# VectorE normalises the tile two slots ahead in front of a slot's activation

## What is computed

```
x = x + 0.5 * ffn(layernorm(x))
x = x + rec(layernorm(x))
x = x + 0.5 * ffn(layernorm(x))

def ffn(x):                                   # 8 experts, top 1
    p = softmax(x @ Wr + br); e = argmax(p); gate = max(p)
    h = relu((norm(x) * ln_g + ln_b) @ W1[e] + b1[e])      # 256 -> 1024
    return (h @ W2[e] + b2[e]) * gate                      # 1024 -> 256

def rec(x):                                   # in 64 features
    x = x @ down_w.T
    for l in range(3):
        c = causal convolution of 4 taps(x)
        r, i = sigmoid(c @ Wr.T + br), sigmoid(c @ Wi.T + bi)
        a = exp(8 * r * log_sigmoid(log_a))
        h_t = a_t * h_(t-1) + sqrt(1 - a_t^2) * i_t * c_t
        x = rms_norm(h @ out_w.T) * norm_w
    return x @ up_w.T
```

## Time and profile before

| | before |
|---|---|
| time of the runs, median | 835.54 us (833.80 to 836.45) |
| the profiled execution's own time | 837.64 us |
| its span in the profile | 835.8 us |
| TensorE matmul busy | 724.3 us, 87% |
| VectorE busy | 393.5 us, 47% |
| ScalarE busy | 266.0 us, 32% |
| GpSimd busy | 194.1 us, 23% |
| mean granted TensorE clock | 0.969 |

### The profile page before, as it was taken

One profiled execution on the slowest core, in us unless ns is written; L12 is line 12 of the kernel. 1 busy time (PEld: TensorE's weight loads), 2 busy tenths in 40 slices (PEclk: granted clock), 3 DMA queues, 4 the chain that ended last, 5 costly groups with the idle time before them and its releaser, 6 DMA issues.

```text
span 835.8 us, 16437 instructions
## 1 busy us (share of the span) xinstructions
PE 724.3 (87%) x4704; PEld 636.1 (76%) x4704; DVE 393.5 (47%) x1248; ACT 266.0 (32%) x670; POOL 194.1 (23%) x193
## 2 busy tenths in 40 slices
PE   5304998999979999999984999999995779999993
PEld 4204986999969878987863887888785669999993
DVE  5401465333326666677641475767774223332331
ACT  3102241222222455563400236566241122222220
POOL 4530136311112211111562130111057011111110
PEclk9999998999999999999988999999998889999998
DMA  6984575875546333342446443433324534555520
GB/s 215 324 271 160 182 232 172 258 233 197 206 140 245 133 126 128 127 138 107 122 164 215 141 162 126 135 133 118 121 90 146 178 127 143 184 187 180 190 70 10
DMA packets 65217, 136.58 MB, mean 163 GB/s; under 512 B 9157, under 2 KB 40146, under 8 KB 64980
## 3 DMA queue, kind: packets, MB, share of 16 engines
q1 hardware_dynamic: 57620, 118.37, 42.3%
q0 software_dynamic: 7488, 16.93, 5.8%
HBM read 114.10 MB, written 24.84 MB: 166 GB/s over the span
## 4 chain that ended last, share of the span: by engine, by line
PE 77%; issue 7%; SPq 6%; DVE 5%; DVEq 2%; DMA 1%; another core or an unknown queue 1%; POOL 0%; POOLq 0%
PE bank L1343 34%; PE bank L1356 30%; PE bank L1245 3%; PE bank L1330 2%; PE bank L1194 2%; SPq L346 2%; SPq L386 2%; PE bank L1250 1%; PE bank L1255 1%; PE bank L1273 1%; DMA w<-in_L_ffn_W 1%; PE bank L1237 1%; DVE act_t L908 1%; DVEq L323 1%
## 5 line engine op out<-in xcount | busy, mean ns | idle before, releaser
L1343 PE MATMUL bank<-mn_t,w 128*128 128x128 f32 x2592 | 319.9, 279 | 12.6 <-issue 12.6
L1343 PEld LDWEIGHTS bank<-mn_t,w 128*128 128x128 f32 x2592 | 307.8, 196 | 21.4 <-issue 21.2
L1356 PE MATMUL bank<-w,act_t 128*128 x1296 | 305.0, 387 | 9.7 <-DVE res L921 5.6
L1356 PEld LDWEIGHTS bank<-w,act_t 128*128 128x128 f32 x1296 | 244.4, 194 | 50.8 <-issue 20.3
L908 DVE TENSOR_SCALAR act_t<-bank,vec 128x128 f32<-128x128 f32 x324 | 91.2, 344 | 188.2 <-PE bank L1343 171.4
L1101 ACT ACTIVATE mn_t<-bank,vec 128x128 f32<-128x128 f32 x162 | 65.2, 452 | 343.7 <-PE bank L1330 282.3
L1111 ACT ACTIVATE act_t<-bank,vec 128x128 f32<-128x128 f32 x324 | 92.6, 369 | 94.0 <-PE bank L1343 81.7
L530 POOL DMA_INDIRECT out_x<-res,pay x40 | 40.8, 1020 | 278.1 <-DVE res L921 277.5
L530 POOL DMA_INDIRECT x_middle<-res,pay x41 | 41.9, 1021 | 268.1 <-DVE res L921 267.2
L915 DVE TENSOR_TENSOR y_b<-bank,b_all 128x256 f32<-128x256 f32 x81 | 34.4, 424 | 130.8 <-PE bank L1356 107.1
L1330 PE MATMUL bank<-ident,mn 128*128 128x128 f32 x162 | 32.8, 285 | 62.6 <-DVE mn L901 41.5
(11 more groups left out here) (157 smaller groups left out, 402.8 us busy)
## 6 DMA issues: line engine op xcount, KB each, us to landing
w<-in_L_ffn_W SPq DMA_DIRECT2D x89, 1024.0 KB
pay<-routed_rows SPq DMA_DIRECT2D x81, 130.0 KB, 2.1
routed_rows<-fill SPq DMA_DIRECT2D x4, 1040.0 KB, 6.2
rows<-in_L_attn_h SPq DMA_DIRECT2D x8, 512.0 KB, 4.8
rows<-x_middle SPq DMA_DIRECT2D x8, 512.0 KB, 6.2
b_all<-in_L_ffn_b SPq DMA_DIRECT2D x1, 1024.0 KB
routed_rows<-rows,dest POOLq DMA_INDIRECT x64
x_middle<-res,pay POOLq DMA_INDIRECT x41, 3.6
```

Of the source, the lines that this page charges most:

```text
L1343: last = t.matmul(b_hid[n][:, c % 4 * P:(c % 4 + 1) * P], w1[i % W1S][:, k * F + c * P:k * F + (c + 1) * P], mn_t[p % 2][i % 2][:, k * P:( ...
L1356: last = t.matmul(b_out[i % 2], act_t[i % 2][:, c * P:(c + 1) * P], w2[:, ds(eb * (WE // FC) + c * D, D)], start=c == 0, stop=c == FC - 1)
```

## The change

VectorE's `norm(p, i + 2)` is called behind `finish(p, i - 2)` and ahead of the work beside the slot and of `activate(p, i)`, in all slots; in the first seven slots it gets an `If` block of its own. The ticks of the other work are new in many places.

```diff
--- before.py
+++ after.py
@@ -21,45 +21,45 @@
 
 SUB = 8
 LN_POW = [40, 48]
-LN_NORMALISE = [96, 112]
+LN_NORMALISE = [96, 120]
 DOWN = [504, 552]
 KEEP_DOWN = [121, 137]
-LN_MOMENTS = [[72, 80], [88, 104]]
+LN_MOMENTS = [[80, 81], [88, 104]]
 LN_TRANSPOSE = [[440, 464], [505, 528]]
 LN_KEEP = [[112, 120], [128, 136]]
-UP = [[1090, 1104], [1112, 1144]]
-ADD = [[273, 275], [280, 288]]
-TAP = [[129, 138], [184, 185], [233, 240]]
-CONVOLVE = [[128, 136], [185, 192], [233, 240]]
-GATES = [[553, 584], [768, 784], [960, 992]]
-TANH = [[139, 152], [192, 200], [241, 248]]
-GATE_INPUT = [[144, 152], [193, 200], [248, 256]]
-ROOT = [[153, 160], [201, 208], [249, 264]]
-SCAN = [[160, 161], [208, 216], [257, 264]]
-PROJECT = [[672, 688], [872, 897], [1064, 1089]]
-SQUARES = [[168, 169], [216, 225], [265, 273]]
-NORMS = [[689, 704], [896, 913], [1088, 1096]]
-RMS_ROOT = [[170, 176], [224, 232], [272, 280]]
-INVERSE = [[176, 177], [224, 232], [272, 274]]
-SPREAD = [[712, 728], [912, 952]]
-RESCALE = [[178, 184], [225, 234]]
+UP = [[1080, 1105], [1112, 1136]]
+ADD = [[272, 274], [280, 282]]
+TAP = [[129, 138], [177, 184], [232, 235]]
+CONVOLVE = [[128, 136], [178, 184], [226, 248]]
+GATES = [[553, 584], [736, 768], [944, 1032]]
+TANH = [[139, 152], [185, 192], [234, 264]]
+GATE_INPUT = [[144, 152], [192, 200], [240, 264]]
+ROOT = [[153, 154], [200, 201], [248, 266]]
+SCAN = [[153, 160], [208, 216], [256, 265]]
+PROJECT = [[656, 681], [864, 889], [1048, 1088]]
+SQUARES = [[168, 170], [216, 224], [265, 272]]
+NORMS = [[680, 697], [888, 912], [1072, 1104]]
+RMS_ROOT = [[169, 176], [217, 233], [267, 280]]
+INVERSE = [[168, 177], [224, 227], [266, 273]]
+SPREAD = [[696, 728], [896, 945]]
+RESCALE = [[176, 179], [225, 232]]
 R_POW = [[56, 57], [144, 145], [144, 145]]
-R_LOGITS = [[504, 552], [1161, 1200], [1161, 1200]]
-R_KEEP_LOGITS = [[128, 138], [296, 299], [296, 299]]
-R_TURN_LOGITS = [[528, 568], [1176, 1216], [1176, 1216]]
+R_LOGITS = [[504, 552], [1152, 1176], [1152, 1176]]
+R_KEEP_LOGITS = [[128, 138], [288, 297], [288, 297]]
+R_TURN_LOGITS = [[528, 568], [1160, 1192], [1160, 1192]]
 R_CHOOSE = [[128, 144], [296, 312], [296, 312]]
-R_EXP = [[137, 152], [300, 320], [300, 320]]
-R_RANKS = [[553, 616], [1208, 1288], [1208, 1288]]
+R_EXP = [[137, 152], [304, 320], [304, 320]]
+R_RANKS = [[553, 616], [1216, 1288], [1216, 1288]]
 R_PLACE = [[136, 152], [304, 320], [304, 320]]
-R_MOMENTS = [[[104, 112], [113, 120]], [[281, 289], [290, 297]], [[281, 289], [290, 297]]]
-R_SCATTER = [[[64, 72], [80, 88]], [[152, 160], [161, 168]], [[152, 160], [161, 168]]]
-R_TRANSPOSE = [[[440, 464], [472, 529]], [[1120, 1145], [1160, 1177]], [[1120, 1145], [1160, 1177]]]
-R_KEEP = [[[112, 120], [129, 136]], [[281, 288], [297, 298]], [[281, 288], [297, 298]]]
+R_MOMENTS = [[[104, 112], [120, 121]], [[281, 288], [289, 290]], [[281, 288], [289, 290]]]
+R_SCATTER = [[[64, 72], [80, 81]], [[152, 160], [161, 168]], [[152, 160], [161, 168]]]
+R_TRANSPOSE = [[[440, 464], [472, 529]], [[1120, 1137], [1153, 1161]], [[1120, 1137], [1153, 1161]]]
+R_KEEP = [[[112, 120], [129, 136]], [[281, 282], [289, 296]], [[281, 282], [289, 296]]]
 R_COUNTS = [648, 1320, 1320]
-R_TABLES = [160, 328, 328]
+R_TABLES = [168, 328, 328]
 LAYER_COLUMNS = 48
 EXP_LOG_A = 56
-LOG_SIGMOID = 56
+LOG_SIGMOID = 64
 
 
 
@@ -940,15 +940,17 @@
                             finish(p, i - 2)
                     elif i >= 2:
                         finish(p, i - 2)
+                    if i < DYN:
+                        with dve.If(used > SLOTS - 1 - i):
+                            norm(p, i + 2)
+                    elif i + 2 < SLOTS:
+                        norm(p, i + 2)
                     beside(p, 2 * i)
                     if i < DYN:
                         with dve.If(used > SLOTS - 1 - i):
                             activate(p, i)
-                            norm(p, i + 2)
                     else:
                         activate(p, i)
-                        if i + 2 < SLOTS:
-                            norm(p, i + 2)
                     beside(p, 2 * i + 1)
                 if p == 0:
                     begin(1)
```

## The result

| | before | after |
|---|---|---|
| median, us | 835.77 (826.66 to 846.85, 20 runs) | 841.12 (834.21 to 844.16, 20 runs) |
| ratio after/before | | 1.0077, 95% interval 1.0047 to 1.0106 |
| profiled execution, us | 837.64 | 839.0 |
| its span, us | 835.8 | 837.3 |
| mean granted clock | 0.969 | 0.929 |

The kernel got slower by 0.8%, beyond the 0.3% that a measurement of it can tell. The forecast was no change at 836.3 us; 841.1 us lies inside its range, but the time moved beyond the measurement's interval where the forecast had no change.

The account below looks back on a forecast made before the run. TensorE was taken to bound the kernel, losing time only at second slots and crawls. The terms -7.04 - 0.49 + 8.3 = +0.8 us gave 836.3 us on the median, no change, range 827 to 842 us.

Parts of the forecast that it names:

- The move of the normalise: Second slot of each phase: input transposes no longer wait for the normalise, -7.04 us, plus -0.49 us in phase 0.
- late next: Second half of the following first products waits for VectorE's activation: some 1.2 us, against 2.0 us of other TensorE work.
- The new places at 0: Other work moved to new ticks on TensorE and VectorE: cost 0, bounds 0 to +2 us.
- scatter place: GpSimd, phase 0: scatters from [80, 88] to [80, 81] make a separate run of 9 issues, +8.3 us.
- The argument from busy time: Mixed slots of phases 1 and 2: TensorE almost always busy, so no idle time to win; activation has over 4 us slack.
- the line of the prediction itself: GpSimd runs of issues: a run of 9 costs 8.2 or 8.3 us, each further issue 1.1 us.
- rival D: Phase 1 or phase 0's new run: a store joins eight scatters, run of 14, 5.4 us more, 841.7 us; chance 0.16.
- Rows and branches: VectorE: waits for rows cost 0, up to 2 us per slot; 28 branch steps cost 0, at most 5.6 us.
- Case B: Phase 0: no crawl for the new run of scatters, 828.0 us or up to 830, faster; chance 0.30.
- the rule from the Trainium skill: Straight code streams ahead, so by it the longer scatter run would cost nothing; the forecast held the timeline against it.

Follow-up runs that it names:

- first set: Four kernels taking the change apart (normalise move, new places, scatter place), run on one chip beside the kernel before, which took 811.51 us there.
- before_again: The kernel before, unchanged, profiled again in the second set of runs: 811.51 us, ratio 1.0007.
- after_third: The kernel after, unchanged, run again where the kernel before took 840.14 us: 840.56 us, ratio 1.0041.
- the pair of the fourth set: The kernel after, unchanged, 840.56 us, and the same with phase 0's scatters back at ticks [80, 88] instead of [80, 81], 832.72 us.
- spread_second: Kernel before with only the normalise moved and each phase's four groups of scatters in four different slots: 829.88 us, ratio 0.9892.
- the pause: Kernel after with a drain and a 2.9 us power operation on GpSimd behind every four scatters: 880.93 us, ratio 1.052.

## Why the prediction was wrong, and where it was right

**The move of the normalise** was right in mechanism and size: forecast 7.04 us at four places, measured 1.90 + 1.83 + 1.75 + 1.94 = 7.42 us. What was called late next, the second half of the first products, waits 0.29 us in phase 1, once. Alone, it is 0.9903 where there are crawls. In the first set, without them, it is 0.9862; the intervals overlap, so that it is worth more there is not shown, though two more transposes wait for the normalise in `before_again`.

**The new places at 0** is the step that failed, and it turned the direction. The bounds were 0 to +2 us. In the profiled pair of the case the sum of 0.8 us became 5.0: the scatter place gave 1.2 us of the difference, the move -0.4 us, and all that the forecast had put at nothing 3.4 us net; its largest parts are 2.03 us in the mixed slots of phase 1 and 2.92 us in the stretch behind them. In the first set, where crawls play no part, the new places with the normalise behind cost 0.7% (5.5 us, interval 3.3 to 7.7), and with the move, and the old scatter place, 806.25 against 799.53 us, 6.7 us. The profiles of that last pair are 9.5 us apart and say where: 1.8 us in the mixed slots, 4.9 us in the stretches behind phases 1 and 2, 1.8 us up to the end of phase 0, 1.6 us in the first two slots of phase 2, the rest -0.6. The argument from busy time ("no idle time to win, and slack of over 4 us") looked at the activation, which had slack; the finish, which frees the bank of the second products, had none: TensorE waits for it 11.3 us instead of 5.6. That is shown for the moments (1.2 us in one slot); how far each of the other moved places contributes, and what delays the stretches behind the phases, was not tried. Where crawls occur, the split is less certain: 832.72 against 830.73 us, ratios whose intervals overlap.

**The scatter place** was right in mechanism and roughly in size. The text took a separate run of 9 at 8.3 us and argued that the next store would come late. In the profiled execution a store came in time on the near side (at 133.28 us) and joined the new run to the old one: 18 issues. The price follows the line of the prediction itself, 8.3 + 9 x 1.1 = 18.2 us against 17.7 measured; the loss over before is 17.7 - 8.2 = 9.5 us, not 8.3. That is rival D's mechanism (a store that joins) at one of its two places, at the front of the run instead of its end. It does not happen each time: in `after_third` the runs are 9 and 10, and the crawl of 10 costs 14.64 - 7.25 = 7.4 us. So the term was 7.4 to 9.5 us against 8.3 forecast: with the move and this place alone the kernel would have stayed within 0.3% of before. That it came so near is in part luck: the price per issue was read as a property of the run, and it isn't one. It is 0 in two of the five comparisons, and in phase 2 of the changed kernel a run of 9 lost 12.9 us.

**Rows and branches.** Between 249 and 426 us the moved normalise waits for rows twice, 2.59 us at 261.47 and 0.34 us at 266.46, in phase 2's mixed slots never; the slots of TensorE around the two keep their 7.25 us, so the cost is 0 as forecast. The 28 branches cost nothing that any run shows, since the move alone gained what was worked out without them.

**Case B** (no crawl for the new run, 828 us) came true in two sets as to the crawl, and for another reason than it named: there no run had a crawl, the first one included. Even so the kernel gained only 0.27% and not B's 0.9%. The eight scatters delay a store and the read behind it, so that TensorE waits 2.49 and 3.34 us more, where B had taken 2 us; and the new places cost their share.

On the rule from the Trainium skill, "Runtime: NRT & Kernel Launch", section "Instruction fetch mechanics" (straight code streams and hardly stalls): the forecast drew from it that the scatter place should change nothing. The pair of the fourth set speaks against that by 7.8 us; in the first two sets, with up to 20 issues and no stall, it held. What failed is the conclusion and not the rule: it speaks of fetching code, and the crawl does not look like a wait for code. The trace of the kernel after has, of all DMA packets, only two instruction packets in the stretch from 126.54 to 151.27 us, of 8 KB each, at 131.29 and 139.61 us; they took 0.31 and 0.61 us, and neither lands when the crawl ends at 146.56.

**Open.** Why the same kernel takes 811.5 us in two sets and 836 to 840 us in the rest. It is not the program, and the data are the same. It need not be the chip either: the first and the fourth set ran on a chip of the same number, 6, and the kernel before took 811.51 us in the one and 840.14 us in the other. No experiment here separates chip, condition and time. The crawl of phase 0 is a small part of it: of the 22.4 us between the spans of `before` and `before_again` the four slots around that crawl have 2.9, the start of phase 0 6.0, and the stretches behind phases 1 and 2, with the long runs there, 15.8; the rest is -2.3. Nor is it settled what TensorE's "issue" time and the held VectorE and ScalarE wait for: the traces tie it to GpSimd's runs of issues in time and by removal, not to a resource.

## What to carry to other kernels

Take a change apart before you judge it: here the edit to the order was worth 1%, and the places that came with it gave all of it back and more. Where the order allows it for nothing, leave a gap between groups of five GpSimd DMAs: in phase 0, gaps of 1.70 to 3.10 us in front of groups of five or six kept them free, and a gap of 1.30 us in phase 1 of `spread_second` did not. Don't buy the gap with a drain or with later transfers. For each thing moved on an engine ask for the slack of every result behind it, the bank that a finish frees as well as the operand that is used next.

## What the hardware did that was not expected

- The kernel before, unchanged, has medians of 811.51, 811.51 and 811.19 us in two sets and 835.77, 839.53 and 840.14 us in the others: 3%, more than any edit of the case but the pause. A number from one chip at one time can't be set beside one from another; ratios within a set can.
- The same run of GpSimd issues stalls TensorE, VectorE and ScalarE for 8 to 18 us in one set and not at all in another. Where it stalls, in phase 0, 5 or 6 issues are free, 9 or 10 cost 6.9 to 8.3 us, and 18 cost 17.7. Runs close behind another don't keep to this: nine issues 1.01 us behind four lost 12.9 us in phase 2 of the kernel after.
- TensorE's granted clock falls during and behind a crawl. Over 126.5 to 151.3 us of the kernel after it is 0.68 on the mean, between the two levels; over the corresponding stretch of `before_again` it is 1.00, the 2.4 GHz level:

```profile
126.50:151.30 24.80, 12.61 (x52) 8.82 (x51) 4.94 (x21) 1.95 (x6) 13.71 (x15) 0.68 0.65 209
```

TensorE is busy half of that time; the row says nothing of which came first.
- A drain of GpSimd behind four indirect DMAs takes 1.8 to 8.1 us, where the DMAs' own issue takes 0.97 us each.
